# Nyquist bin on token partitions with small float32 products, and a third tree with fetched leaves

## Chip, cores and metric

The kernel runs on one core of a Trainium2 chip. The metric is device microseconds of one execution, the median of several runs.

## The reference, cut to what matters

```python
x = x + attn(layernorm(x))            # x: (2, 4096, 512)
x = x + ffn(layernorm(x))
# attn: q, k, v = unit_projection(x @ W.T + b), unit_projection(v) = ifft(fft(v) / (|fft(v)| + 1e-8)).real
#       s = cumsum(bind(k, v), axis=1); out = ifft(fft(s) * conj(fft(q))).real
# ffn:  logits = x @ W_in.T + b_in    # 8 trees of 255 nodes, depth 7
#       each tree is walked from its root, right where the logit is positive; only the 8 nodes on
#       the way keep silu(logit), the others are zero; out = masked @ W_out.T
```

In the frequency domain the attention is elementwise. Its 512 real inputs give 255 complex bins and two real ones, bin 0 and bin 256. Bin 256 is called the Nyquist bin, or in the code before `special` and `sp_`.

## The kernel before, in words

8192 tokens go through in 32 blocks of 256 (`T`), each as two halves of 128 tokens (`J` = 2). `steps` runs a set-up (`first`), the first block, a loop over blocks 1 to 30 and the last block. Every engine has its instructions in an order written out by hand in its own `step(i, attn, nxt)`; block i's feed-forward part is interleaved with the attention part of block n = i + 1 and with the first layer norm of block n + 1. Engines synchronise by semaphores, and each executes strictly in its order.

TensorE (`step`, L597): `project` for Q, K and V (L477, 144 products of 256 columns); `logits` of eight trees (L507), each in up to two column groups of 128 nodes, twelve products of 256 columns a group; `counts` (L517), which adds to a tree's logits a large negative number for every node off the path, from the decisions `dec`; `leaf_rows_of` (L526); `down` for both token halves (L542, products of 512 columns; three for every column group); and `inverse_transform` of block n (L477, bank_i). The float32 values are split into fp16 high and low halves, hence three products each.

Trees in `GATHERED` (0 and 1) have only their inner nodes in the dense product, `DENSE` = 14 column groups in all. Their one leaf for each token is found by `leaf` (L709), `leaf_rows_of` and `leaf_row_copy` (L720), fetched by an indirect DMA on GpSimd (`fetch`, L1027), multiplied with the token on VectorE (`leaf_dots`, L1199), passed through silu (`leaf_silu`, L730) and added (`leaf_add`, L1209).

The Nyquist bin lies before on single partitions: ScalarE's `evac_im` (L684 to L688) writes row 32q of `sp_raw`, 256 tokens along the row. VectorE adds eps (L1123), inverts (L1125), multiplies (`special_unit`, L1131, L1134), scans (`special_sum`, L1154) and splits (`special_product`, L1166 to L1170); TensorE adds it to the inverse transform by two one-row products for each half (`tab_sp`, in L477).

Around these VectorE does the `residual` (L1222 to L1234), the statistics and normalisation of layer norm (L1056 to L1088), the reciprocals of q and of k times v (L1098, L1110), `decide` (L1179, from logits to `dec`), `act_low` (L1186, the low halves of activations), the scans (L1142, L1145) and `result` (L1240). ScalarE evacuates projections, squares, takes roots (L701), does `silu` (L742) and `act_high` (L752). GpSimd does `sum_squares` (L935), `add_eps`, `q_unit`, `bind` (L958 to L961), `unbind` (L968 to L971), `z_sums`, `z_low` (L983) and the fetches. SyncE transposes normalised tokens by DMA (`xt` for the projections, `x2t` for the logits).

## Time and profile before

| what | us |
|---|---|
| median of 3 runs | 1993.65 |
| lowest, highest | 1991.71, 1995.52 |
| the profiled execution | 1992.84 |
| its span, first to last instruction | 1991.0 |

A block is read in the timelines from one first product of Q's projection to the next. The profile has 39541 instructions; the mean granted TensorE clock is 0.987 of full. Matmuls are pipelined: the timeline prints the length of each instruction or group, but what one costs TensorE is the distance from its start to the start of the next. "Idle" in brackets is the time that the engine sat idle before, with what ended it.

### The profile page before, as it was taken

The numbers are of one execution on the slowest core, as the hardware profiler recorded it, in microseconds if no ns is written. First come the engines' busy times: TensorE is split into PE (matmuls) and PEld (weight loads), VectorE is DVE, ScalarE is ACT, GpSimd is POOL, SyncE is SP. The second block draws the span as 40 slices with busy tenths as digits, with TensorE's granted clock in tenths as the row PEclk, the third lists the DMA queues.
The fourth block names the chain that finished last, engine by engine and source line by source line (L and its number), as shares of the span: only waits on it lengthen the run. The fifth ranks groups of instructions, "written<-read, shape, count | busy, mean of one in ns | idle before, by whom it ended". The sixth has DMA issues, their size and how long they took to land.

```text
span 1991.0 us, 39541 instructions
## 1 busy us (share of the span) xinstructions
PE 1868.4 (94%) x14360; PEld 1362.3 (68%) x14360; DVE 1744.3 (88%) x2900; ACT 1131.1 (57%) x2150; POOL 945.9 (48%) x744
## 2 busy tenths in 40 slices
PE   8489999999999999999999999999999999999978
PEld 6367766677766667766667776667776666776655
DVE  4988899988899889899988889998889998889983
ACT  5565555566555566555556555556655555655533
POOL 1354454554444554445555445455444555544540
PEclk9699999999999999999999999999999999999998
DMA  8022232222232222223222223222223322222312
GB/s 272 11 75 76 74 95 74 74 84 74 74 95 91 67 79 76 78 84 95 65 83 84 74 74 95 74 74 90 69 74 95 93 65 79 79 76 83 85 54 64
DMA packets 181642, 163.05 MB, mean 82 GB/s; under 512 B 140146, under 2 KB 140658, under 8 KB 181618
## 3 DMA queue, kind: packets, MB, share of 16 engines
q1 hardware_dynamic: 163186, 95.35, 16.6%
q0 software_dynamic: 18432, 67.38, 10.9%
q8 instruction: 15, 0.25, 0.1%
q14 instruction: 9, 0.07, 0.0%
HBM read 95.58 MB, written 16.78 MB: 56 GB/s over the span
## 4 chain that ended last, share of the span: by engine, by line
DVE 57%; issue 16%; PE 9%; POOL 5%; ACT 4%; DMA 2%; DVEq 1%; SPq 1%; POOLq 0%; ACTq 0%
DVE arena L1186 9%; PE bank_l L507 7%; DVE sp_hat L1131 6%; DVE arena L1209 4%; DVE arena L1199 4%; DVE sp_den L1125 3%; DVE dec L1179 3%; DVE xn_pair L1088 2%; DVE sp_cum L1154 2%; DMA arena<-xn_pair 2%; DVE arena L1142 2%; DVE st L1056 2%; DVE sp_den L1123 2%; DVE arena L1145 2%; DVE arena L1110 2%
## 5 line engine op out<-in xcount | busy, mean ns | idle before, releaser
L507 PE MATMUL bank_l<-arena,win_mem 128*128 128x256 f16 x5376 | 625.7, 273 | 27.4 <-DMA arena<-xn_pair 27.4
L542 PE MATMUL bank_l<-wout_mem,arena 128*128 128x512 f16 x2688 | 590.8, 379 | 0.3 <-DVE arena L1186 0.3
L507 PEld LDWEIGHTS bank_l<-arena,win_mem 128*128 128x128 f16 x5376 | 522.0, 98 | 96.5 <-issue 19.1
L477 PE MATMUL bank_p<-arena,wf_hi 128*128 128x256 f16 x3072 | 508.5, 273 | 18.0 <-DMA arena<-xn_pair 9.9
L542 PEld LDWEIGHTS bank_l<-wout_mem,arena 128*128 128x128 f16 x2688 | 263.0, 98 | 304.0 <-DVE arena L1186 0.8
L477 PE MATMUL bank_p<-arena,wf_lo 128*128 128x256 f16 x1536 | 419.3, 273 | 0.0
L935 POOL TENSOR_TENSOR arena<-arena 128x512 f32<-128x512 f32 x96 | 121.7, 1268 | 617.7 <-ACT arena L697 617.7
L477 PEld LDWEIGHTS bank_p<-arena,wf_hi 128*128 128x128 f16 x3072 | 296.1, 98 | 65.1 <-ACT arena L688 16.7
L742 ACT ACTIVATE arena<-bank_l,bias_in,s_logit 128x256 f32<-128x256 f32 x448 | 225.8, 558 | 168.1 <-PE bank_l L517 167.7
L1186 DVE SCALAR_TENSOR_TENSOR arena<-arena,s_act 128x512 f16<-128x512 f32 (+1 forms) x256 | 252.5, 1006 | 39.6 <-ACT arena L752 39.5
L1179 DVE TENSOR_SCALAR dec<-bank_l,thr,off 128x256 bf16<-128x256 f32 x256 | 131.9, 527 | 64.5 <-PE bank_l L507 64.2
L1027 POOL DMA_INDIRECT arena<-in_leaf_rows,leaf_row x128 | 149.2, 1166 | 66.0 <-ACT leaf_row L720 36.5
L752 ACT ACTIVATE arena<-arena,s_act 128x512 f16<-128x512 f32 (+1 forms) x256 | 162.7, 662 | 1.0
L477 PEld LDWEIGHTS bank_p<-arena,wf_lo 128*128 128x128 f16 x1536 | 150.6, 98 | 17.7
L730 ACT ACTIVATE leaf_act<-leaf_dot,arena 128x1 f32<-128x1 f32 x128 | 30.7, 287 | 230.1 <-DVE arena L1199 230.1
L958 POOL TENSOR_TENSOR arena<-arena 128x512 f32<-128x512 f32 x31 | 44.2, 1426 | 189.9 <-DVE arena L1116 189.9
L517 PE MATMUL bank_l<-dec,path 128*128 128x256 bf16 x512 | 98.7, 274 | 37.1 <-DVE dec L1179 33.5
L1131 DVE TENSOR_TENSOR sp_hat<-sp_raw,sp_den 1x256 f32<-1x256 f32 x93 | 124.0, 1333 | 0.8
L677 ACT ACTIVATE arena<-bank_p,bias_f 128x256 f32<-128x256 f32 x192 | 80.0, 468 | 70.5 <-PE bank_p L477 70.5
L1110 DVE RECIPROCAL arena<-arena 128x256 f32<-128x256 f32 x64 | 111.7, 1747 | 1.1
L983 POOL TENSOR_TENSOR arena<-arena 128x512 f16<-128x512 f32 x62 | 98.0, 1601 | 23.1 <-ACT arena L665 23.1
L1098 DVE RECIPROCAL arena<-arena 128x256 f32<-128x256 f32 x64 | 107.6, 1721 | 0.0
(180 smaller groups left out, 2722.3 us busy)
## 6 DMA issues: line engine op xcount, KB each, us to landing
arena<-in_x SPq DMA_DIRECT2D x32, 512.0 KB, 3.6
arena<-arena SPq DMA_DIRECT2D x32, 512.0 KB, 2.9
out<-arena SPq DMA_DIRECT2D x64, 256.0 KB, 2.1
wout_mem<-in_w_in_t SPq DMA_DIRECT2D x1, 3584.0 KB, 15.1
arena<-in_w_out_t SPq DMA_DIRECT2D x1, 3584.0 KB, 14.1
arena<-xn_pair SPq DMA_TRANSPOSE x128, 2.7
arena<-in_leaf_rows,leaf_row POOLq DMA_INDIRECT x128, 4.9
win_mem<-in_wq SPq DMA_DIRECT2D x1, 1024.0 KB, 8.3
```

The source lines that it names most:

```text
L477: mm = pe.matmul(bank, a, b, start=(n == 0), stop=(n == len(pairs) - 1))
L507: mm = pe.matmul(bank_l[t % 4][:, c * T:(c + 1) * T], a[:, k, w:w + P], x2t[:, :, b, k, :], start=(c == 0 and k == 0 and m == 0), stop=((t ...
L542: mm = pe.matmul(bank_l[j][:, :], a[:, m, tok], w[:, m, :], start=(m == 0 and a is a_hi and w is wout_hi), stop=(m == DENSE - 1 and a is a ...
L742: ins = act.activation(acts[:, t % HELD, c * T:(c + 1) * T], bank_l[t % 4][:, c * T:(c + 1) * T], ACT.Silu, bias=bias_in[:, c, t:t + 1], s ...
L752: act.activation(a_hi[:, m:m + wide, :], acts[:, t % HELD, 0:wide * T].rearrange("p (c t) -> p c t", c=wide), ACT.Copy, scale=s_act[:, 0:1 ...
L935: pool.tensor_tensor(mag[:, q].rearrange("p c t -> p (c t)"), sq[:, 0:2].rearrange("p c t -> p (c t)"), sq[:, 2:4].rearrange("p c t -> p ( ...
L1027: pool.indirect_dma_start(fetched[:, g, j, :], None, leaf_rows, bass.IndirectOffsetOnAxis(leaf_row[:, g, j:j + 1], 0)).then_inc(leaf_fetch ...
L1098: dve.reciprocal(mag[:, Q, h], mag[:, Q, h]).then_inc(rinv_ready, 1)
L1110: dve.reciprocal(mag[:, V, h], mag[:, V, h]).then_inc(kv_rinv_ready, 1)
L1131: ins = dve.tensor_tensor(sp_hat[0:1, q, :], sp_raw[s, :], sp_den[s, :], ALU.mult)
L1179: dve.tensor_scalar(dec[:, t % HELD, :], bank_l[t % 4][:, 0:T], thr[:, t:t + 1], off[:, 0:1], ALU.is_gt, ALU.mult).then_inc(dec_ready, 1)
L1186: dve.scalar_tensor_tensor(out=a_lo[:, m, :], in0=acts[:, t % HELD, 0:wide * T].rearrange("p (c t) -> p c t", c=wide), scalar=s_act[:, 0:1 ...
```

## The change

A third tree (2) goes to `GATHERED`; `DENSE` becomes 13, and its leaves have a fetch round of their own (`leaf_rows_of(i, 1)`, `leaf_row_copy(i, 1)`, `fetch(i, 2)`, `leaf_dots(i, 2)`, `leaf_silu(i, 2)`, `leaf_add(i, 2)`). The Nyquist bin is turned by TensorE onto token partitions, [128 tokens, 2 halves, 3], by two float32 products on `sp_raw` (`nyquist_rows`); size, eps, inverse, unit and product are six-element instructions; its running sum is five float32 products with an upper triangle and a full matrix (`nyquist_sums`). It no longer goes through the inverse transform: `residual` adds it per token as a scalar, added on even and subtracted on odd positions, for which the columns are sorted by parity. The four one-row products of `tab_sp` go. The orders on TensorE, ScalarE, GpSimd and VectorE are written anew.

```diff
-GATHERED = (0, 1)
+GATHERED = (0, 1, 2)
 LEAVES = len(GATHERED)
-ROUNDS = ((0, 1),)
+ROUNDS = ((0, 1), (2,))
...
-        tab_sp = sb("tab_sp", [1, QI + 2], F16)
+        running = sb("running", [P, 2 * P + 3])
+        upper, full, row_of = running[:, 0:P], running[:, P:2 * P], running[0:96, 2 * P:2 * P + 3]
...
                         f = (2 * part + c) * P
                         pairs = []
 
             def logits(i, t, c):
 
+                if c == 0 and t == 0:
+                    pe.wait_ge(x2t_ready, 16 * J * (i + 1))
...
+            def nyquist_rows(n):
+
+                pe.wait_ge(raw_im, 3 * n + 3)
+                if not isinstance(n, int) or n:
+
+                    pe.wait_ge(x1_ready, J * n)
+                for j in range(J):
+                    mm = pe.matmul(sp_rows[:, j, :], sp_raw[:, j * P:(j + 1) * P], row_of, start=True, stop=True)
+                mm.then_inc(sp_rows_full, 1)
+
+            def nyquist_sums(n):
+
+                pe.wait_ge(sp_kv_ready, n + 1)
+                pe.matmul(sp_sums[:, 0:1], upper, sp_kv[:, 0:1], start=True, stop=True)
+                pe.matmul(sp_sums[:, 1:2], upper, sp_kv[:, 1:2], start=True, stop=False)
+                pe.matmul(sp_sums[:, 1:2], full, sp_kv[:, 0:1], start=False, stop=True)
+                pe.matmul(sp_sums[:, 2:3], full, sp_kv[:, 0:1], start=True, stop=False)
+                pe.matmul(sp_sums[:, 2:3], full, sp_kv[:, 1:2], start=False, stop=True).then_inc(sp_sums_full, 1)
...
+                if rnd:
+                    pe.wait_ge(leaf_row_ready, len(ROUNDS) * i + rnd)
...
-                        if t == LEAVES:
+                        if t == 3:
...
+            def transform_back(i):
+
+                n = i + 1
+                pe.wait_ge(z_hi_ready, 2 * n + 2)
+                pe.wait_ge(z_lo_ready, 2 * n + 2)
+
+                pe.wait_ge(leaf_row_ready, len(ROUNDS) * (i + 1))
+                pe.wait_ge(sp_carry_ready, n + 1)
+                for j in range(J):
+                    pe.wait_ge(x1_ready, J * i + j + 1)
+                    inverse_transform(j)
...
-                    if c == 0:
-                        pairs += [(sp_z_hi[:, tok], tab_sp[:, :]), (sp_z_lo[:, tok], tab_sp[:, :])]
...
+                nyquist_rows(0)
...
-
-                    pe.wait_ge(xt_ready, 16 * J * (n + 1))
-                    pe.wait_ge(raw_im, 3 * n)
                     project(n, Q)
                     project(n, K)
                     project(n, V)
...
+                    nyquist_rows(n)
+                logits(i, 0, 0)
+                logits(i, 1, 0)
+                counts(i, 0)
+                logits(i, 2, 0)
+                logits(i, 3, 0)
+                logits(i, 3, 1)
+                logits(i, 4, 0)
+                logits(i, 4, 1)
+                counts(i, 1)
+                if attn:
+                    nyquist_sums(n)
+                leaf_rows_of(i, 0)
+                counts(i, 2)
+                counts(i, 3)
+                logits(i, 5, 0)
+                logits(i, 5, 1)
+                leaf_rows_of(i, 1)
+                logits(i, 6, 0)
+                counts(i, 4)
+                logits(i, 6, 1)
+                logits(i, 7, 0)
+                counts(i, 5)
+                logits(i, 7, 1)
+                counts(i, 6)
+                down(i, 0)
+                down(i, 1)
+                if attn:
+                    transform_back(i)
...
+            def nyquist_size(n):
+
+                act.wait_ge(sp_rows_full, n + 1)
+                act.activation(sp_size, sp_rows, ACT.Abs).then_inc(sp_abs_ready, 1)
...
+                if q == Q and (not isinstance(n, int) or n):
+
+                    act.wait_ge(sp_rows_full, n)
...
+                act.activation(root_warm[:, :], ln_eps[:, :], ACT.Sqrt)
                 if attn:
                     evac_re(n, Q)
                     evac_im(n, Q)
+                    evac_re(n, K)
                     square(n, Q)
-                    evac_re(n, K)
                 std(i, mv2, rs2, ln2_mv, ln2_std)
                 if attn:
-                    root(n, Q)
+                    evac_im(n, K)
                 if attn:
 
...
-                    evac_im(n, K)
+                    root(n, Q)
+                    evac_re(n, V)
                     square(n, K)
-                    evac_re(n, V)
+                    evac_im(n, V)
                     root(n, K)
-                    evac_im(n, V)
+                    nyquist_size(n)
                     square(n, V)
-                if isinstance(i, int) and i == 0:
-
-                    act.wait_ge(ffn_consts_done, 1)
-                leaf(i, 0)
-                if attn:
                     root(n, V)
                 if nxt:
                     std(n + 1, mv1, rs1, ln1_mv, ln1_std)
-                if attn:
-                    sp_magnitude()
-                leaf(i, 1)
+                if isinstance(i, int) and i == 0:
+
+                    act.wait_ge(ffn_consts_done, 1)
+                leaf(i, 0)
...
                 silu(i, 0)
+                act_high(i, 0)
+                leaf(i, 1)
                 silu(i, 1)
+                leaf_row_copy(i, 0)
+                leaf(i, 2)
                 silu(i, 2)
-                act_high(i, 0)
                 act_high(i, 1)
+                act_high(i, 2)
                 silu(i, 3)
-                act_high(i, 2)
                 act_high(i, 3)
-                leaf_row_copy(i, 0)
-                silu(i, 4)
-                act_high(i, 4)
-                silu(i, 5)
-                silu(i, 6)
-                act_high(i, 5)
...
+                silu(i, 4)
+                silu(i, 5)
+                act_high(i, 4)
+                act_high(i, 5)
+                silu(i, 6)
+                silu(i, 7)
+                act_high(i, 6)
                 act_high(i, 7)
+                leaf_silu(i, 0)
+                leaf_row_copy(i, 1)
                 if attn:
                     z_high(n)
-                leaf_silu(i, 0)
                 leaf_silu(i, 1)
-                if attn:
-                    act.activation(root_warm[:, :], ln_eps[:, :], ACT.Sqrt)
+                leaf_silu(i, 2)
...
+                    add_eps(n, K)
+                    sum_squares(n, V)
                     q_unit(n)
-                    sum_squares(n, V)
...
                     z_sums(n)
+                fetch(i, 2)
+                if attn:
                     z_low(n, 0)
                     z_low(n, 1)
...
+            def nyquist_den(n):
 
                 dve.wait_ge(sp_abs_ready, n + 1)
-                dve.tensor_scalar(sp_den[:, :], sp_den[:, :], eps_sp[:, 0:1], None, ALU.add).then_inc(spd_ready, 1)
...
+                dve.tensor_tensor(sp_den[:, :, :], sp_size, eps_sp[:, :, :], ALU.add).then_inc(sp_den_ready, 1)
+
...
+            def nyquist_unit(n):
+
                 dve.wait_ge(sp_inv_ready, n + 1)
...
+                dve.tensor_tensor(sp_hat[:, :, :], sp_rows, sp_den[:, :, :], ALU.mult).then_inc(sp_hat_ready, 1)
+
+            def nyquist_bind(n):
+
                 dve.wait_ge(sp_hat_ready, n + 1)
-                dve.tensor_tensor(sp_kv[:, :], sp_hat[:, K, :], sp_hat[:, V, :], ALU.mult).then_inc(sp_kv_ready, 1)
+                dve.tensor_tensor(sp_kv[:, :], sp_hat[:, :, K], sp_hat[:, :, V], ALU.mult).then_inc(sp_kv_ready, 1)
+
+            def nyquist_unbind(n):
+
+                dve.wait_ge(sp_sums_full, n + 1)
+                dve.scalar_tensor_tensor(out=sp_z[:, :], in0=sp_sums[:, 0:J], scalar=sp_carry[:, 0:1],
+                                         in1=sp_hat[:, :, Q], op0=ALU.add, op1=ALU.mult).then_inc(sp_z_ready, 1)
+
+            def nyquist_carry(n):
+
+                dve.wait_ge(sp_z_ready, n + 1)
+                dve.tensor_scalar(sp_carry[:, :], sp_sums[:, J:J + 1], sp_carry[:, 0:1], keep[:, bass.ds(n + 1, 1)],
+                                  ALU.add, ALU.mult).then_inc(sp_carry_ready, 1)
...
+            def carries(n):
+
                 dve.wait_ge(cum_ready, n + 1)
-                dve.wait_ge(sp_cum_ready, n + 1)
-
-                kp = keep[:, bass.ds(n + 1, 1)]
-                dve.tensor_scalar(carry[:, :], cum[:, :, T - 1], kp, None, ALU.mult).then_inc(carry_ready, 1)
-                dve.tensor_scalar(sp_carry[:, :], sp_cum[:, T - 1:T], keep[0:1, bass.ds(n + 1, 1)], None,
+                dve.tensor_scalar(carry[:, :], cum[:, :, T - 1], keep[:, bass.ds(n + 1, 1)], None,
                                   ALU.mult).then_inc(carry_ready, 1)
...
                 cos, sin = xn2[:, j, 0:2 * QI], xn2[:, j, 2 * QI:4 * QI]
                 xj, edge = x1[:, j, :], 4 * QI
-                dve.tensor_tensor(cos[:, 0:QI], ce[:, 0:QI], co[:, 0:QI], ALU.add)
-                dve.tensor_tensor(cos[:, QI:], ce[:, 0:QI], co[:, 0:QI], ALU.subtract)
+                dve.wait_ge(sp_z_ready, i + 1)
+                top, odds, evens = sp_z[:, j:j + 1], slice(0, ODDS), slice(ODDS, QI)
+                for part, sign in ((odds, ALU.subtract), (evens, ALU.add)):
+                    up, down = cos[:, part], cos[:, QI + part.start:QI + part.stop]
+                    dve.scalar_tensor_tensor(out=up, in0=ce[:, part], scalar=top, in1=co[:, part], op0=sign, op1=ALU.add)
+                    dve.scalar_tensor_tensor(out=down, in0=ce[:, part], scalar=top, in1=co[:, part], op0=sign,
+                                             op1=ALU.subtract)
...
                     wout_low(3)
                 if attn:
                     q_inverse(n, 0)
-                    q_inverse(n, 1)
                 if nxt:
                     next_stats(n + 1)
+                if attn:
+                    nyquist_den(n)
+                    nyquist_inverse(n)
+                    nyquist_unit(n)
                 decide(i, 0)
-                decide(i, 1)
-                if attn:
+                if attn:
+                    q_inverse(n, 1)
                     kv_denominator(n)
                     kv_inverse(n, 0)
+                    kv_inverse(n, 1)
+                    nyquist_bind(n)
+                    k_scale(n)
+                decide(i, 1)
                 decide(i, 2)
-                if attn:
-                    kv_inverse(n, 1)
-                    k_scale(n)
+                decide(i, 3)
                 act_low(i, 0)
-                decide(i, 3)
                 decide(i, 4)
-                act_low(i, 1)
-                act_low(i, 2)
-                act_low(i, 3)
-                decide(i, 5)
-                decide(i, 6)
-                if attn:
-                    running_sum(n)
-                act_low(i, 4)
                 if nxt:
                     scale_and_shift(n + 1)
+                if attn:
+                    nyquist_unbind(n)
+                decide(i, 5)
+                act_low(i, 1)
+                if attn:
+                    running_sum(n)
+                act_low(i, 2)
+                decide(i, 6)
+                if attn:
+                    nyquist_carry(n)
+                act_low(i, 3)
                 decide(i, 7)
+                act_low(i, 4)
                 act_low(i, 5)
-                if attn:
-                    special_inverse(n)
                 act_low(i, 6)
                 act_low(i, 7)
-                if attn:
-                    special_unit(n)
+                leaf_dots(i, 0)
+                leaf_add(i, 0)
                 if nxt:
                     low_of(n + 1, 0, xn1, xn1_hi_ready, xn1_lo_ready)
-                if attn:
-                    special_sum(n)
-                leaf_dots(i, 0)
-                if attn:
-                    special_product(n)
-                if nxt:
                     low_of(n + 1, 1, xn1, xn1_hi_ready, xn1_lo_ready)
                 leaf_dots(i, 1)
-                leaf_add(i, 0)
+                if attn:
+                    carries(n)
                 leaf_add(i, 1)
+                leaf_dots(i, 2)
+                leaf_add(i, 2)
                 result(i, 0)
                 result(i, 1)
 
```

## Rows read from the trace of the kernel before

**Rows 1.** The page: busy us (share of the span) and instructions of each engine.

```profile
PE 1868.4 (94%) x14360; PEld 1362.3 (68%) x14360; DVE 1744.3 (88%) x2900; ACT 1131.1 (57%) x2150; POOL 945.9 (48%) x744
```

**Rows 2.** Windows, 200 to 1800 us: engines busy us; granted clock (1.00 full).

```profile
200.00:1800.00 1600.00, 1545.49 (x12015) 1125.14 (x12014) 1445.40 (x2383) 925.85 (x1789) 805.64 (x626) 1.00 0.27 80
```

**Rows 3.** TensorE timeline, one block: start us, us, line, operation [idle <-releaser].

```profile
986.47 0.39 PE L477 MATMUL bank_p<-arena,wf_hi 128*128 128x256 f16 x2 [0.43 <-DMA arena<-xn_pair]
...
1002.43 0.27 PE L477 MATMUL bank_p<-arena,wf_lo 128*128 128x256 f16 x1
1003.24 0.39 PE L507 MATMUL bank_l<-arena,win_mem 128*128 128x256 f16 x2 [0.53 <-DMA arena<-xn_pair]
...
1020.71 0.39 PE L517 MATMUL bank_l<-dec,path 128*128 128x256 bf16 x2 [0.21 <-DVE dec L1179]
...
1023.77 1.46 PE L542 MATMUL bank_l<-wout_mem,arena 128*128 128x512 f16 x6
1025.99 0.39 PE L517 MATMUL bank_l<-dec,path 128*128 128x256 bf16 x2 [0.75 <-DVE dec L1179]
...
1043.05 0.22 PE L477 MATMUL bank_i<-tab_hi,arena 128*128 128x129 f16 x1
...
1045.62 0.39 PE L477 MATMUL bank_p<-arena,wf_hi 128*128 128x256 f16 x2 [0.41 <-DMA arena<-xn_pair]
```

**Rows 4.** The same timeline, the inverse transform of one token half.

```profile
1043.16 0.22 PE L477 MATMUL bank_i<-tab_hi,arena 128*128 128x129 f16 x1
1043.32 0.23 PE L477 MATMUL bank_i<-tab_sp,sp_z_hi 1*128 1x129 f16 x1
...
1043.53 0.23 PE L477 MATMUL bank_i<-tab_hi,arena 128*128 128x128 f16 x1
```

**Rows 5.** Waits of TensorE, 200 to 1800 us: total us, times, longest us.

```profile
PE bank_l L517 <- DVE dec L1179: 27.5, 50, 0.8
...
PE bank_l L507 <- DMA arena<-xn_pair: 9.4, 27, 0.7
PE bank_p L477 <- DMA arena<-xn_pair: 9.2, 22, 0.4
```

**Rows 6.** TensorE timeline, set-up: small float32 products (a call is x2).

```profile
5.38 0.57 PE L434 MATMUL bank_p<-b_pair,arena 128*128 128x6 f32 x2
5.81 0.57 PE L429 MATMUL bank_p<-b_pair,arena 128*128 128x6 f32 x2
...
20.91 0.28 PE L443 MATMUL bank_l<-mx,arena 128*128 128x5 f32 x2
21.05 0.68 PE L455 MATMUL bank_i<-arena 128*128 128x257 f32 x2
```

**Rows 7.** ScalarE timeline: evacuation of Q's imaginary part after its last product.

```profile
991.92 0.47 ACT L684 ACTIVATE sp_raw<-bank_p,bias_f 1x256 f32<-1x256 f32 x1 [1.78 <-PE bank_p L477]
...
992.74 0.45 ACT L688 ACTIVATE arena<-bank_p,bias_f 128x256 f32<-128x256 f32 x1
```

**Rows 8.** VectorE groups, whole span: busy us, mean ns | idle before.

```profile
L1131 DVE TENSOR_TENSOR sp_hat<-sp_raw,sp_den 1x256 f32<-1x256 f32 x93 | 124.0, 1333 | 0.8
...
L1125 DVE RECIPROCAL sp_den<-sp_den 96x256 f32<-96x256 f32 x32 | 56.0, 1749 | 1.1
...
L1123 DVE TENSOR_SCALAR sp_den<-sp_den,eps_sp 96x256 f32<-96x256 f32 x32 | 43.1, 1347 | 0.4 <-ACT sp_den L835 0.4
```

**Rows 9.** VectorE timeline: low halves of activations, GpSimd busy, then idle.

```profile
1016.74 3.46 DVE L1186 SCALAR_TENSOR_TENSOR arena<-arena,s_act 128x512 f16<-128x512 f32 x2 [1.11 <-ACT arena L752]
...
1023.61 0.72 DVE L1186 SCALAR_TENSOR_TENSOR arena<-arena,s_act 128x512 f16<-128x512 f32 x1
```

**Rows 10.** VectorE timeline: first instruction of the residual.

```profile
1048.56 0.29 DVE L1222 TENSOR_TENSOR arena<-bank_i,odd 128x127 f32<-128x127 f32 x1 [0.29 <-DVE arena L1240]
```

**Rows 11.** GpSimd timeline: second fetch of leaves; low half of z.

```profile
1029.80 1.25 POOL L1027 DMA_INDIRECT arena<-in_leaf_rows,leaf_row  x1 [0.15 <-issue]
...
1035.60 3.05 POOL L983 TENSOR_TENSOR arena<-arena 128x512 f16<-128x512 f32 x2 [0.74 <-ACT arena L665]
```

192 lines of the change are left out of this document (76 added, 116 removed).

## The prediction

> **What bounds the kernel now.** I read the page's busy shares first: TensorE 94%, VectorE 88% [rows 1]. The stretch from 200 to 1800 us shows the steady state: TensorE is busy 1545 of 1600 us, VectorE 1445, at full clock [rows 2]. Then I read one block in TensorE's timeline [rows 3], from the first product of Q's projection at 986.47 to the next one at 1045.62: 59.15 us. The reader is to see that products follow one another almost without a gap, with four small idle spots: 0.70 us between the last projection product (1002.43 plus one step of 0.11) and the first logits (1003.24), which wait for the transposed tokens; 0.21 and 0.75 us ahead of `counts`, which wait for a decision on VectorE; 0.41 us ahead of the next projection, again for transposed tokens. The waits view gives them over 27 blocks: 27.5 us for decisions, or 1.0 a block, and 9.4 and 9.2 us for the two transposes [rows 5]. So TensorE is the bound; VectorE, second at 90%, causes most of the gaps. What TensorE is spared is gained, unless VectorE's or another engine's new order takes it back.
>
> **The change part by part, for one block.** The sum is made on TensorE.
>
> Logits: one column group less, 12 products. 143 steps of projection, same shape, take 1002.43 - 986.47 = 15.96 us, 0.11 each [rows 3]; so -1.3 us. Down: 84 products become 78. From 1023.77 to 1043.05 are 19.28 us; less 0.75 of stall and 0.22 of `counts` that is 18.31, or 0.218 each; so -1.3. The one-row products: from 1043.16 to 1043.53 [rows 4] the last ordinary product and the two of them take 0.37 us, where an ordinary one takes about 0.06 (two from 1043.05 [rows 3] to 1043.16); 0.31 for each half, -0.6 for both. Two more leaf-row products: at most an ordinary 0.06 each, +0.1.
>
> Five float32 products for the sums. The trace has small ones in the set-up only. At 5.38 a call with six columns takes 0.43 us to the next, at 20.91 one with five columns takes 0.14 [rows 6]. The second was preceded by a wait, in which its weights could be loaded; the first ones follow one another, but at the very start. These are the ends: 0.7 to 2.2 us for five. I take 0.21, as the 20.91 one is at the clock of the steady state, and a back-to-back call can't hide its second load: +1.05.
>
> The Trainium skill speaks against this part: "TensorE: Matmul & The Clock Gate", section on weight-path perf modes, says that the fast weight load does not apply to fp32 weights; and "FP8 and Floating Point Precision", TensorE Precision Notes, has true fp32 as four passes. The doubled instructions of the rows fit in kind, while two instructions a call are not four. By a full unhidden load the price would be that of the upper end, the rival named below.
>
> `nyquist_rows` sits between projection and logits and waits for ScalarE to evacuate V's imaginary part. For Q this evacuation starts at 991.92 and its third instruction starts at 992.74 and lasts 0.45 [rows 7]; Q's last product ends near 991.8 (48 steps of 0.11 after 986.47), so the data are there 1.4 us after it; with the semaphore 1.5. Then come two float32 calls, 0.4. Against today's gap of 0.70 that is +1.2. Ends: +0.9 if ScalarE is quicker, +2.2 if `square(n, K)`, ahead of it in its queue, runs late. Behind this wait stand all logits. The wait for transposed tokens, which ends the gap now, is hidden under it as long as VectorE's chain from the inverse transform to the transposes isn't over 1.3 us later.
>
> That chain: `residual` starts at 1048.56 now [rows 10], 3.5 us after the inverse transform's end, since VectorE is behind. The change takes three unit products of 1.33 us, an inversion of 1.75 and an addition of 1.35 [rows 8] from it, with the scan and splits some 10 us a block, and gives back an estimated 1.5 us of six-element instructions, four operations on 128x512 for `leaf_dots` and `leaf_add` at some 0.7 each as the shorter one in [rows 9], and an estimated 0.3 to 1.1 for the residual, whose two 0.29 us operations for each half [rows 10] become four of half the length. VectorE falls from 53 (0.903 of 59.15 [rows 2]) to about 47 us a block. Costed at nothing on the path: it is hidden by TensorE, as is the third leaf on ScalarE; SyncE's queue keeps its order. The transposes of the next block's tokens come earlier, as their low halves no longer stand behind the Nyquist work: the 0.34 us stall (9.2 us over 27) goes.
>
> The stalls at `counts`, 1.0 us a block, go in their present places: `counts(7)` now has three trees, not two, of `down` ahead of it, and the others are a group later. New ones come. VectorE's new order puts both inversions of k and v (as long as that of [rows 8], 3.5 us) and k's scaling ahead of `decide(1)`; worked through with present durations, `decide(1)` ends about 0.65 us after TensorE wants it for `counts(1)`. And five `act_low` (trees 3 to 7) and `decide(7)` must fit between the scans and the end of the first half of `down`. One takes 0.72 us when GpSimd is idle, 1.73 beside its `bind` (3.46 for two) [rows 9]; TensorE takes 1.3 a tree. I take 0.35 of stall, bounds 0 and 1.8. GpSimd gets a third fetch (1.25 plus about 1.1 and gaps, 2.7 us) ahead of `z_low`, which now ends at 1038.65, 4.4 us before it is needed [rows 3, 11]; `down` ends 1 to 2 us sooner, so near 1 us of cover is left. Cost nothing; if `bind` starts over 1 us later, every further us counts.
>
> The Trainium skill's "GPSIMD Engine Reference", table of specifications, says that GpSimd shares SBUF interfaces with VectorE, where the latter has two SBUF inputs. The 0.72 against 1.73 agrees. It leaves the new products with a PSUM input alone.
>
> Sum: -1.3 - 1.3 - 0.6 + 0.1 + 1.05 + 1.2 = -0.85; -0.34 - 1.0 of stalls gone, +0.65 + 0.35 new: -1.2 a block. With 31 blocks -37 us.
>
> Ends of the run: the last block has no attention; it gains logits and down, 2.6. In the set-up the addition and the inversion stand once on the path to the first inverse transform (1.35 + 1.75 by the means) [rows 8], about -3 with the small ones that replace them and the smaller weights to split. Together -43; 1992.84 - 43 = 1949.8. The median of the runs is 0.8 above the profiled execution: 1950.
>
> **The rivals.**
>
> A, the forecast: 1950, by its stalls of about 1 us a block 1935 to 1965.
>
> B, no new stall: both new ones vanish, since VectorE has 7 us a block to spare and can be ahead of TensorE. 31 x 1.0 less: 1919. For it speaks the idle time that VectorE gains; against it that GpSimd's instructions stretch VectorE's.
>
> C, starved `down`, on the slower side: `silu(7)` waits for `act_low(4)`, `act_high(6)` stands behind `silu(7)`, and `act_low(6)` behind that. If each `act_low` costs 1.73 beside GpSimd's `unbind` and fetches, the five stretch 5 us beyond the short ones; what `down` can't hide is 1.8 us, and with z then late behind the third fetch 1 more. Against the 0.35 that is +2.45 a block: 1950 + 76 = 2026. It decides from 1.4 us above my stalls; up to there the change still gains. For it: the 1.73. Against: the 0.72, whenever GpSimd happens to wait.
>
> D, loads of float32 weights unhidden: 0.43 for each of seven calls, +1.5 a block: 1950 + 48 = 1998, no change. For it the row at 5.38; against it the clock and place of that row.
>
> E, the evacuation is not the end of that wait, but the transposes, by a residual that is 1.1 us longer: +0.3 to 0.8 a block, 1960 to 1975. Still faster.
>
> **How the numbers follow.** A 0.45, B 0.22, C 0.13, D 0.08, E 0.12. Range 1915 to 1998: from B with some block terms smaller, to D; C lies outside and a tail below B. A measurement of this kernel can tell 0.2%, 4 us, from no change. Faster: A, B, E and a little of D, 0.80; same: half of D and a sliver of C, 0.05; slower 0.15.
>
> **What would show each step right or wrong.** TensorE's timeline: first logits about 2 us after V's last product, released by ScalarE; the float32 group of five about 1.05 us long; `down` starting at once, and `counts(7)` without wait. The waits view: decisions under 1.0 us a block together with waits for L1186's successor. VectorE busy about 47 of 58. GpSimd's `z_low` ends before `down` does. The block from projection to projection near 57.9 us. Wrong would be: waits of `down` for low halves over 1 us a block, or the inverse transform waiting for GpSimd.

## The result, and the profile after

The changed kernel takes 2117.1 us (median of 4, 2111.4 to 2121.3), the one before 1992.7 (median of 4 on the same chip): ratio 1.063, 95% interval 1.059 to 1.066. It is 124 us slower where 43 us less were forecast.

From the page of the kernel after, the busy line of the engines and the two DMA kinds (number, median us from issue to landing), then its steady state and three shorter stretches as windows (columns as in [rows 2]; the last three are granted clock, DMA engines' busy share and GB/s):

```profile
PE 1881.7 (89%) x14168; PEld 1400.7 (66%) x14168; DVE 1623.7 (77%) x3066; ACT 1116.6 (53%) x2247; POOL 987.7 (47%) x800
```

```profile
arena<-xn_pair SPq DMA_TRANSPOSE x128, 3.8
arena<-in_leaf_rows,leaf_row POOLq DMA_INDIRECT x192, 6.1
```

```profile
200.00:1900.00 1700.00, 1545.15 (x11792) 1149.92 (x11791) 1332.17 (x2505) 906.40 (x1857) 835.81 (x673) 0.95 0.40 91
1039.90:1058.20 18.30, 16.07 (x144) 13.93 (x144) 15.20 (x40) 12.81 (x28) 3.22 (x3) 1.00 0.37 106
1058.20:1064.00 5.80, 4.87 (x31) 3.82 (x32) 2.77 (x8) 2.51 (x5) 1.96 (x2) 0.71 0.15 27
1103.00:1107.00 4.00, 3.92 (x21) 2.90 (x22) 3.23 (x6) 2.62 (x6) 0.00 (x0) 0.57 0.00 0
```

Against [rows 1, 2]: 192 instructions less, and yet TensorE is busy longer; its idle share rises from 3.4% to 9%; the granted clock falls from 1.00 to 0.95, and the last two rows show where: behind waits of TensorE, where the mean of the stretch lies between the two levels (1.2 and 2.4 GHz), 0.71 and 0.57 of 2.4. It does not happen behind every wait: the row from 1039.90 starts behind one of 2.96 us and stands at 1.00. The DMA engines' busy share rises from 0.27 to 0.40 with 14% more bytes a second. VectorE falls only from 53 to 49.5 us a block (1332.17 of 1700, times 63.13), not to 47.

The waits of the kernel after, 200 to 1900 us, 27 blocks (total us, times, longest us):

```profile
DVE arena L1236 <- DMA arena<-in_leaf_rows,leaf_row: 107.8, 27, 5.7
PE bank_p L480 <- DMA arena<-xn_pair: 105.4, 27, 5.6
PE bank_i L551 <- ACT arena L740: 44.0, 27, 1.9
PE bank_l L530 <- DMA arena<-xn_pair: 4.1, 7, 0.9
```

The waits for decisions in [rows 5] have gone. In their place TensorE waits 3.9 us a block for the transposed tokens of the next block (0.34 before), and 1.6 for V's imaginary part. The same in TensorE's timeline, one block:

```profile
1039.95 0.39 PE L480 MATMUL bank_p<-arena,wf_hi 128*128 128x256 f16 x2 [2.96 <-DMA arena<-xn_pair]
1058.23 0.60 PE L551 MATMUL bank_i<-running,sp_raw 96*128 96x3 f32 x4 [1.94 <-ACT arena L740]
1059.73 4.18 PE L530 MATMUL bank_l<-arena,win_mem 128*128 128x256 f16 x24 [0.90 <-DMA arena<-xn_pair]
1063.97 6.71 PE L530 MATMUL bank_l<-arena,win_mem 128*128 128x256 f16 x60
1070.75 0.28 PE L557 MATMUL bank_i<-sp_kv,running 128*128 128x1 f32 x2
...
1071.57 0.36 PE L561 MATMUL bank_i<-sp_kv,running 128*128 128x1 f32 x2
1103.08 0.39 PE L480 MATMUL bank_p<-arena,wf_hi 128*128 128x256 f16 x2 [3.62 <-DMA arena<-xn_pair]
```

From projection to projection 63.13 us, 3.98 more than in [rows 3]; times 31 that is 123, the whole loss. In this block, by the terms of the prediction: the wait ahead of the projection +3.2 (3.62 for 0.41; forecast -0.34); from the end of V's last product (1056.13) to the logits 3.60 for 0.70, so +2.9 (forecast +1.2); the first 24 logits products take 4.02 us (to 1063.75), not the 2.6 that 24 of the sixty behind them take, +1.4 (not forecast); the float32 group +1.04 (from 1070.75 to 1071.57 and a call of 0.22); waits at `counts` and `down` -1.0; work removed -3.2, as forecast. That makes 4.4; 0.4 is unassigned. This block is one of the slower ones at the logits. Over the 13 blocks from 600 to 1400 us the first 24 products of the projection take 2.63 us in four blocks and 3.8 to 5.1 in nine of them; the first 24 of the logits 2.6 in five and 3.9 to 4.3 in eight: 2.2 us a block more than at the full clock.

Why the transposes are late shows on GpSimd, SyncE and VectorE just ahead of that block (the third pair of fetches and `z_low` behind it, the transposes' issue, VectorE):

```profile
1028.05 1.23 POOL L1063 DMA_INDIRECT arena<-in_leaf_rows,leaf_row  x1 [0.16 <-POOL arena L1027]
1029.58 0.95 POOL L1063 DMA_INDIRECT arena<-in_leaf_rows,leaf_row  x1 [0.30 <-issue]
1030.55 2.27 POOL L1034 TENSOR_TENSOR arena<-arena 128x512 f16<-128x512 f32 x2
```

```profile
1029.80 3.51 SPq L339 DMA_TRANSPOSE arena<-xn_pair  x2
```

```profile
1024.48 0.68 DVE L1236 SCALAR_TENSOR_TENSOR arena<-arena 128x512 f32<-128x512 f32 x1
...
1030.24 3.13 DVE L1236 SCALAR_TENSOR_TENSOR arena<-arena 128x512 f32<-128x512 f32 x1
...
1039.03 0.69 DVE L1236 SCALAR_TENSOR_TENSOR arena<-arena 128x512 f32<-128x512 f32 x1 [3.00 <-DMA arena<-in_leaf_rows,leaf_row]
...
1044.31 0.28 DVE L1263 SCALAR_TENSOR_TENSOR arena<-bank_i,sp_z,odd 128x64 f32<-128x64 f32 x1 [0.41 <-DVE arena L1284]
```

The transposes are issued 1.8 us behind the first gather of the third pair, and the last of both kinds land near 1039, some 9 us after their issue (9.3 for the second gather, 8.7 and 9.3 for the transposes; the first gather takes 5.3). VectorE waits for the fetch, and the residual begins at 1044.31, 7.3 us after the end of the inverse transform (1039.95 less 2.96), against 3.4 before by the same reckoning ([rows 10] less 1045.21 of [rows 3]). How long the transposes take from issue to landing (minimum, median, maximum over 200 to 1900 us), first before, then after; half of them are those of `xn2`, which meet no fetch:

```profile
DMA to landing us min/median/max: 2.7/2.8/4.2
```

```profile
DMA to landing us min/median/max: 3.1/5.4/12.0
```

### The profile page after: what moved, and what is told of

Read it like the earlier page. It is cut to its first block, busy times and chain, and to the rows that moved or that the text cites. A ratio compares the mean times of both kernels' runs of the same rounds, so it can differ in the third digit from the quotient of the medians.

```text
span 2109.6 us, 40048 instructions
## 1 busy us (share of the span) xinstructions
PE 1881.7 (89%) x14168; PEld 1400.7 (66%) x14168; DVE 1623.7 (77%) x3066; ACT 1116.6 (53%) x2247; POOL 987.7 (47%) x800
## 4 chain that ended last, share of the span: by engine, by line
PE 56%; DMA 16%; DVE 9%; issue 6%; ACT 6%; SPq 2%; POOL 1%; DVEq 0%; ACTq 0%; POOLq 0%
PE bank_l L530 27%; PE bank_p L480 21%; DMA arena<-xn_pair 13%; PE bank_l L590 3%; PE bank_l L540 3%; DMA arena<-in_leaf_rows,leaf_row 3%; DVE arena L1236 2%; SPq L339 2%; DVE arena L1246 2%; ACT arena L794 1%; DVE arena L1223 1%; DVE xn_pair L1126 1%; ACT arena L804 1%; ACT arena L738 1%; ACT sp_raw L736 1%
## 5 line engine op out<-in xcount | busy, mean ns | idle before, releaser
L480 PE MATMUL bank_p<-arena,wf_hi 128*128 128x256 f16 x3072 | 554.8, 288 | 117.1 <-DMA arena<-xn_pair 116.1
L530 PEld LDWEIGHTS bank_l<-arena,win_mem 128*128 128x128 f16 x4992 | 498.4, 101 | 95.7 <-DMA arena<-xn_pair 18.6
L590 PE MATMUL bank_l<-wout_mem,arena 128*128 128x512 f16 x2496 | 549.2, 379 | 0.0
L986 POOL TENSOR_TENSOR arena<-arena 128x512 f32<-128x512 f32 x96 | 121.5, 1266 | 697.1 <-ACT arena L749 697.1
L1236 DVE SCALAR_TENSOR_TENSOR arena<-arena 128x512 f32<-128x512 f32 x192 | 199.1, 1072 | 124.6 <-DMA arena<-in_leaf_rows,leaf_row 124.6
L1063 POOL DMA_INDIRECT arena<-in_leaf_rows,leaf_row x192 | 209.8, 1093 | 91.0 <-issue 46.1
L1246 DVE SCALAR_TENSOR_TENSOR arena<-arena,leaf_act 128x512 f32<-128x512 f32 x192 | 194.2, 1052 | 55.5 <-ACT leaf_act L782 55.5
L1223 DVE SCALAR_TENSOR_TENSOR arena<-arena,s_act 128x512 f16<-128x512 f32 (+1 forms) x256 | 215.0, 860 | 28.0 <-ACT arena L804 28.0
L761 ACT ACTIVATE on_leaf<-bank_l,one,off_inv 128x256 f16<-128x256 f32 x96 | 53.9, 561 | 156.7 <-PE bank_l L540 156.6
L991 POOL TENSOR_SCALAR arena<-arena,eps_s 128x512 f32<-128x512 f32 x64 | 46.5, 726 | 130.8 <-ACT arena L753 130.8
## 6 DMA issues: line engine op xcount, KB each, us to landing
wout_mem<-in_w_in_t SPq DMA_DIRECT2D x1, 3328.0 KB, 16.3
```

The lines of the kernel that those rows point to most:

```text
L480: mm = pe.matmul(bank, a, b, start=(n == 0), stop=(n == len(pairs) - 1))
L530: mm = pe.matmul(bank_l[t % 4][:, c * T:(c + 1) * T], a[:, k, w:w + P], x2t[:, :, b, k, :], start=(c == 0 and k == 0 and m == 0), stop=((t ...
L590: mm = pe.matmul(bank_l[j][:, :], a[:, m, tok], w[:, m, :], start=(m == 0 and a is a_hi and w is wout_hi), stop=(m == DENSE - 1 and a is a ...
L986: pool.tensor_tensor(mag[:, q].rearrange("p c t -> p (c t)"), sq[:, 0:2].rearrange("p c t -> p (c t)"), sq[:, 2:4].rearrange("p c t -> p ( ...
L1063: pool.indirect_dma_start(fetched[:, g, j, :], None, leaf_rows, bass.IndirectOffsetOnAxis(leaf_row[:, g, j:j + 1], 0)).then_inc(leaf_fetch ...
L1223: dve.scalar_tensor_tensor(out=a_lo[:, m, :], in0=acts[:, t % HELD, 0:wide * T].rearrange("p (c t) -> p c t", c=wide), scalar=s_act[:, 0:1 ...
```

## Experiments

Theory C (collision): leaf fetches and token transposes in flight together delay each other, and the projection waits behind that. Rival S (series): the third leaf's arithmetic on VectorE makes the residual late. Rival W: the wait ahead of `nyquist_rows` is what costs. Times are medians, with the ratio to the kernel before on the same chip and its 95% interval; a point is one per cent of the time of the kernel before. The lists of waits show the largest rows unless said otherwise.

### e1_low_early: the transposes issued earlier

```diff
@@ VectorE, step @@
                 act_low(i, 4)
+                low_of(n + 1, 0, ...); low_of(n + 1, 1, ...)
                 act_low(i, 5)
...
                 leaf_add(i, 0)
-                low_of(n + 1, 0, ...); low_of(n + 1, 1, ...)
```

> The changed kernel, with VectorE's two low halves of the next block's tokens moved from behind leaf_add(0) to behind act_low(4), so that SyncE issues the token transposes before the second and third leaf fetches are in flight. Theory C (collision: transposes and leaf fetches in flight together delay each other): TensorE's wait ahead of the projection, 3.9 us a block in the changed kernel, falls under 0.5, transposes land in about 3 us, the clock returns towards 1.00, and the time is 1950 to 2010 us. Theory W (the waits and float32 products of the Nyquist part in TensorE's own order cost the time): the order of this pair changes little, 2090 to 2120. Theory S (the third leaf makes VectorE late by itself): the wait ahead of the projection goes, but the one ahead of the logits grows, 2060 to 2110.

2048.9 us, 1.031 [1.024, 1.039]: 3.1 points of the 6.3 are back. The wait of the projection for transposes is gone; 1.3 us a block of waiting for ScalarE (`evac_im`, L740) stand there now, and ScalarE's square root ahead of it waits 3.0 us a block (79.9 over 27) for VectorE, whose residual is late. C's range (1950 to 2010) is missed by 39 us: the collision carries half of the loss, and something else the rest.

### e2_no_third_fetch, e3_nyquist_only, e4_tree_only: the parts alone

e2 puts a `memset` of one column in place of the third fetch (the third tree's leaf is missing from its output). e3 keeps two gathered trees and takes the Nyquist part with the new orders. e4 is the kernel before with the third gathered tree alone, its fetch between `z_sums` and `z_low`.

```diff
@@ e2: GpSimd, fetch @@
-                for j in range(J): pool.indirect_dma_start(fetched[:, 2, j, :], ...)
+                for j in range(J): pool.memset(no_fetch[:, j:j + 1], 0.0)
@@ e3 @@
-GATHERED = (0, 1, 2)
+GATHERED = (0, 1)
```

> The changed kernel without the DMAs of the third leaf fetch (each is a GpSimd memset of one column, and the rows stay zero, so the third tree's leaf is left out of the output); every other instruction is there. Theory C: transposes land in 3 to 4 us, waits ahead of the projection under 0.5 us a block, 1950 to 1990 us. Theory S: also 1950 to 1990, since VectorE no longer waits for the third leaf; C and S are told apart by the run with the early low halves. Theory W: 2090 to 2120, GpSimd being off the path.

> The changed kernel with its Nyquist part and its new orders, but only two gathered trees (14 column groups, two fetches). TensorE has 2.6 us a block more work than in the changed kernel. Theories C and S: no third fetch, so the wait ahead of the projection is small; 1990 to 2040 us. Theory W: the loss of the Nyquist part stays and the dense column comes on top, 2150 to 2210.

> The kernel before with the third gathered tree alone: its Nyquist part and its orders stay as before, the third fetch stands between z_sums and z_low. Theory C: the first of the two transposes, issued near the third fetch, is late, the second is not; VectorE, fuller by 2.5 us a block, is late for the residual: 2000 to 2100 us. Theory W: TensorE is spared 2.5 us a block and nothing is added to it: 1920 to 1950.

e2: 1987.1, 1.000 [0.997, 1.003]. e3: 1992.3, 1.003 [1.002, 1.004]. e4: 2126.9, 1.071 [1.067, 1.074]. The waits of TensorE (200 to 1850 us) of e2, all of them, then the largest of e4:

```profile
PE bank_i L552 <- ACT arena L741: 52.9, 28, 1.9
PE bank_l L531 <- DMA arena<-xn_pair: 20.6, 28, 1.2
```

```profile
PE bank_p L477 <- DMA arena<-xn_pair: 70.8, 26, 4.5
```

Without the third fetch the wait for tokens is not in the list, with the rest of the change in place; with the third tree alone it is. So the third gathered tree loses the time, the Nyquist part neither loses nor gains (W falls as the cause of the loss: its wait of 1.9 us stands in e2 too, at 1.000). e4 lies 27 us above its range of 2000 to 2100; e2 and e3 lie in theirs. e2 says one thing more: it keeps the arithmetic of the third leaf on VectorE and spares TensorE 2.6 us a block, by an estimate 4 points, and still ends level with e3. So in these orders, and without its fetch, the third leaf costs about what it saves.

### e5_low_copy_early, e6_rows_late, e7_all_three

e5 is e1 with `leaf_row_copy(1)` moved ahead of `leaf_silu(0)`, behind `act_high(5)`, so that the third fetch starts earlier. e6 is the changed kernel with `nyquist_rows` behind the first two logits (and ScalarE's and VectorE's share of it moved back). e7 is both.

```diff
@@ e6: TensorE, step @@
                 project(n, V)
-                nyquist_rows(n)
                 logits(i, 0, 0)
                 logits(i, 1, 0)
+                nyquist_rows(n)
```

> The run with early low halves, and ScalarE's leaf_row_copy(1) moved from behind leaf_silu(0) to behind act_high(5), so that GpSimd can issue the third fetch at once after z_sums (it waited 2.6 us there). Theory C+S (both the collision and VectorE's wait for the third leaf cost time): the leaf lands 2.5 us sooner, VectorE reaches the residual 2 to 3 us sooner, the wait ahead of the logits and the wait of the projection for ScalarE (33.6 us over 26 blocks) go; 1.5 to 3 us a block, 1955 to 2005 us. Theory C alone: no more than 0.5 us a block, 2030 to 2050.

> The changed kernel with nyquist_rows moved on TensorE from ahead of the logits to behind the logits of trees 0 and 1, and the size, eps, inverse and unit of the bin moved back with it on ScalarE and VectorE. The wait for V's evacuation (1.9 us a block) and the lower clock in the logits behind it go, unless the transposed tokens end that wait anyway (they came 0.8 us later still in the changed kernel). Theory C: here they do, and the gain is 0 to 0.5 us a block: 2095 to 2120. Theory W: 2 to 3.5 us a block, 2010 to 2050.

> Early low halves, early leaf_row_copy and late nyquist_rows together. If the three losses (collision, VectorE's wait for the third leaf, wait for V's evacuation with its lower clock) add up to the whole distance, TensorE's 2.6 us a block of spared work should show: 1910 to 1960 us, under the kernel before (1986 on this chip). If a further cost of the third leaf stays: 1970 to 2010.

e5: 2035.1, 1.022 [1.018, 1.026], in the range of "C alone" and not in the one that was expected. e6: 2127.8, 1.069 [1.065, 1.072], no gain on the changed kernel and 8 us above C's range: its waits moved from `nyquist_rows` to the logits, which wait for `xn2`'s transposes (63.7 us over 26 blocks). e7: 2019.1, 1.014 [1.011, 1.018], above both of its ranges. What is left in e7, TensorE's largest wait, its timeline, VectorE's and one row of GpSimd's:

```profile
PE bank_l L530 <- DMA arena<-xn_pair: 89.3, 27, 3.7
```

```profile
1012.10 5.30 PE L530 MATMUL bank_l<-arena,win_mem 128*128 128x256 f16 x24 [3.45 <-DMA arena<-xn_pair]
```

```profile
1041.61 3.29 DVE L1239 SCALAR_TENSOR_TENSOR arena<-arena 128x512 f32<-128x512 f32 x1
...
1046.17 3.65 DVE L1249 SCALAR_TENSOR_TENSOR arena<-arena,leaf_act 128x512 f32<-128x512 f32 x2 [0.65 <-ACT leaf_act L784]
...
1058.28 0.28 DVE L1266 SCALAR_TENSOR_TENSOR arena<-bank_i,sp_z,odd 128x64 f32<-128x64 f32 x1 [0.41 <-DVE arena L1287]
```

```profile
1041.86 1.28 POOL L1029 TENSOR_TENSOR arena<-arena 128x512 f32<-128x512 f32 x1
```

Here no transfer is late. The three leaves run one behind another on VectorE from 1041.61 to the results near 1057.9, 16 us, some of it stretched (3.29 us, beside GpSimd's `z_sums`, for a dot product that takes 0.68 by itself), and the logits pay: 3.3 us of waiting a block and then, in eight of the 13 blocks from 600 to 1400 us, 24 products in 3.9 to 5.1 us (5.09 here) in place of 2.6.

### e8_nyquist_rows_late and e9_two_trees_std_early: the Nyquist part made to pay

e8 is e3 with `nyquist_rows` late. e9 adds ScalarE's order for the second norm; it computes everything, with two gathered trees.

```diff
@@ e9: ScalarE, step @@
                     evac_im(n, Q)
-                    evac_re(n, K)
                     square(n, Q)
                 std(i, mv2, rs2, ln2_mv, ln2_std)
-                    evac_im(n, K)
+                    evac_re(n, K)
                 act.wait_ge(xt_ready, 16 * J * (n + 1))
                 high(i, xn2, ln2_done, xn2_hi_ready)
+                    evac_im(n, K)
```

> The run with two gathered trees, and nyquist_rows late as above. There the wait for V's evacuation (1.6 us a block) is the only long wait of TensorE, and tokens are transposed in time. If that wait is the price of the Nyquist part: 0.8 to 1.6 us a block less, 1940 to 1970 us. If the transposed tokens or decide(0) end the wait instead: 1985 to 1995.

> The two-tree kernel with nyquist_rows behind the first logits, and on ScalarE the square root of the second norm (std) and the copy of the high half (high) set ahead of the work on K: order evac_im(Q), square(Q), std, evac_re(K), high, evac_im(K). In the trace of its parent std started 2.4 us after VectorE had the variances (1042.85 to 1045.22), and the logits waited 1.75 us a block for x2's transposes. Theory (the chain residual, norm, transposes ends the wait ahead of the logits, and a queue position on ScalarE is part of it): the wait of the logits goes to below 0.3 us a block, 28 x 1.6 = 45 us less than 1977, so 1925 to 1940. Rival (project(V) waits for evac_im(K) instead, or VectorE's work ends the next wait): the 1.7 us turn up ahead of the projection of V or at the counts, 1965 to 1980.

e8: 1976.9, 0.992 [0.990, 0.995], between its two ranges. e9: 1944.2, 0.981 [0.979, 0.982]: faster than both kernels, 4 us above its range. ScalarE and VectorE in e8, where the square root waits in its queue behind K's evacuation, then ScalarE in e9:

```profile
1045.22 0.29 ACT L696 ACTIVATE rs<-mv,ln_eps 128x2 f32<-128x2 f32 x1
...
1047.46 1.15 ACT L723 ACTIVATE xn_pair<-arena 128x512 f16<-128x512 f32 x2
```

```profile
1045.54 0.17 DVE L1102 RECIPROCAL rs<-rs 128x2 f32<-128x2 f32 x1 [2.70 <-ACT rs L696]
```

```profile
1025.56 0.28 ACT L696 ACTIVATE rs<-mv,ln_eps 128x2 f32<-128x2 f32 x1
1025.86 0.84 ACT L728 ACTIVATE arena<-bank_p,bias_f 128x256 f32<-128x256 f32 x2
1027.38 1.15 ACT L723 ACTIVATE xn_pair<-arena 128x512 f16<-128x512 f32 x2 [0.68 <-DVE arena L1106]
```

In e8 TensorE waits 1.75 us a block for `xn2`'s transposes. In e9 that is gone, and this is all that TensorE waits for between 200 and 1850 us, with the window of its steady state:

```profile
PE bank_l L540 <- DVE dec L1215: 19.7, 28, 0.7
```

```profile
200.00:1800.00 1600.00, 1580.35 (x12620) 1197.65 (x12619) 1312.60 (x2418) 929.45 (x1830) 837.89 (x635) 1.00 0.27 82
```

It is the 0.65 us at `counts(1)` that the prediction worked out, in its place.

### e12_spare_fetch and e14_spare_low_early: the collision by itself

e12 is e8 with a third pair of fetches into a buffer that nobody reads, issued where the changed kernel issues its third (ScalarE's `leaf_row_copy` waits for it, but only in the next block, before it writes the row numbers anew). e14 moves in addition `low_of` of the next tokens as e1 does.

```diff
@@ e12: GpSimd, step @@
                     z_sums(n)
+                for j in range(J):
+                    pool.indirect_dma_start(spare[:, j, :], None, leaf_rows, ...leaf_row[:, 1, j:j + 1]...)
                     z_low(n, 0)
```

> The two-tree kernel with nyquist_rows late (1977), plus a third pair of indirect fetches of the same size, issued where the changed kernel issues its third one, into a buffer that nobody reads: same traffic, no work and no wait on any other engine behind it. Collision theory: the median landing of the transposes rises from 2.7 us to 4 or more, the projection gets a wait for transposed tokens of 1 to 3 us a block, and the time becomes 2010 to 2070. Rival (the transfers share without loss, only VectorE's work for the third leaf costs): transposes stay below 3.2 us and the time within 1 per cent of 1977.

> The two-tree kernel with the spare third pair of fetches (2134, against 1977 without), and the low halves of the next tokens, and so the token transposes, moved ahead on VectorE, from behind the first leaf's addition to behind act_low(4). The fetches are the same, only the transposes start some 8 us sooner. Collision theory: the transposes land in 3 to 3.5 us, the wait of the projection is gone, 1980 to 2010. Rival (the spare fetch costs by itself, through GpSimd's 2.5 us and VectorE beside it, not by meeting the transposes): above 2080.

e12: 2133.7, 1.076 [1.074, 1.079], 8.4 points above e8. e14: 1992.0, 1.002 [1.001, 1.003], 7.5 points below e12 again. The issue of the spare fetch and of the transposes, then the landing of all transposes in the steady state and what TensorE waits for; e12:

```profile
1046.23 1.22 POOL L1073 DMA_INDIRECT spare<-in_leaf_rows,leaf_row  x1 [0.16 <-POOL arena L1030]
```

```profile
1047.98 2.89 SPq L341 DMA_TRANSPOSE arena<-xn_pair  x2
```

```profile
DMA to landing us min/median/max: 2.7/5.6/12.0
```

```profile
PE bank_p L482 <- DMA arena<-xn_pair: 94.7, 26, 4.8
```

and e14, with the same fetches:

```profile
1032.48 1.23 POOL L1073 DMA_INDIRECT spare<-in_leaf_rows,leaf_row  x1 [0.16 <-POOL arena L1030]
```

```profile
1026.09 2.91 SPq L341 DMA_TRANSPOSE arena<-xn_pair  x2
```

```profile
DMA to landing us min/median/max: 2.7/2.7/2.8
```

Last the DMA engines in one block, with two pairs of fetches and one pair of transposes in each: the changed kernel, all of it and from the issue of the transposes on; then e14:

```profile
1022.80:1039.10 16.30, 14.19 (x84) 7.06 (x82) 12.17 (x18) 2.38 (x8) 9.13 (x8) 1.00 0.83 158
1029.80:1039.10 9.30, 7.19 (x52) 3.89 (x49) 5.82 (x9) 0.48 (x2) 2.99 (x3) 1.00 1.09 164
```

```profile
1026.00:1039.50 13.50, 13.17 (x62) 5.82 (x61) 12.51 (x16) 3.64 (x10) 10.28 (x9) 1.00 0.64 195
```

Nobody reads the spare rows and no work in the block stands behind them. The transposes issued 1.8 us behind them take up to 12 us; issued 6.4 us ahead of them, never over 2.8. This shows C: it is neither the traffic nor GpSimd's time, which both remain in e14 (together they cost 0.9 points against e8), but the meeting. The order counts: in e14 the two transposes are issued at 1026.1 and 1027.8 and the second pair of fetches at 1027.3 and 1028.8, as near as in e12, and they are not late. In e12, as in the changed kernel, two pairs of fetches are ahead of them; no run puts them right behind one pair only.

The last three rows show what the mean of 0.40 hides. While both kinds are in flight the 16 engines are full (1.09; the share adds up the times of packets). The bytes are nearly the same, 158 times 16.3 is 2.6 MB and so is 195 times 13.5, but the engines spend 13.5 us on them (0.83 of 16.3) where e14 spends 8.6 (0.64 of 13.5). Together the packets take longer, then; by which mechanism stays open.

The size was missed: 2134 for an expected 2010 to 2070. Against e8 that is 157 us, or 5.1 a block. TensorE waits 3.6 us for the tokens of the projection, where 1 to 3 were expected, and the next 24 products take 1.2 us more than in e8 on average (2.63 to 5.1 us over the 13 blocks from 600 to 1400 us). VectorE's wait for ScalarE's square root grows too, to 7.5 us a block (195.7 over 26, 2.7 in e8), as it stands behind the evacuations of a late projection; TensorE does not feel that, it waits 1.75 us for `xn2`'s transposes in both.

The Trainium skill, "DMA: Bandwidth & Descriptors", section on queues, rings and completion order, says that a DMA engine takes packets from its queues in turn, and that the increment which reports a transfer is written only after all earlier writes of that engine, those of other queues too. The trace agrees in kind: the second gather and the transposes issued near 1029 are reported late, near 1039, while by themselves they land in 2.7 and 4.5 to 5.6 us (e8). No run here tells a late write from a late report of it.

### e10, e11, e13, e15: the series on VectorE

e10 is e7 with e9's ScalarE order. e11 is the changed kernel and e13 is e10, each with the third tree's dot product and addition over one column, not 512 (so that the third leaf is left out of the output but for one column; fetch and waits stay). e15 is e7 with the leaves in the order dots 0, dots 1, add 0, dots 2, add 1, add 2 and `high` ahead of `evac_im(K)`.

```diff
@@ e11, e13: leaf_dots and leaf_add, g == 2 @@
-                    row = fetched[:, g, j, 0:D]
+                    row = fetched[:, g, j, 0:1]
@@ e15: VectorE, step @@
-                leaf_add(i, 0)
                 leaf_dots(i, 1)
+                leaf_add(i, 0)
-                leaf_add(i, 1)
                 leaf_dots(i, 2)
+                leaf_add(i, 1)
                 leaf_add(i, 2)
```

> The three-tree kernel with all three edits (low halves of the next tokens early, leaf_row_copy(1) early, nyquist_rows late), and the same order of std and high on ScalarE as in the two-tree one. Its parent ran at 2019 and waited 3.4 to 3.7 us a block ahead of the logits. Theory: 2 us of that goes and with it part of the slow products behind it: 28 x 2 to 2.8 = 55 to 80 us less, 1940 to 1965; what is left of the wait, 1.4 us, is the third leaf's series on VectorE. Rival (the late residual alone sets it, ScalarE's place doesn't matter since the residual is late): above 2005.

> The changed kernel, but the third tree's dot product and its addition on VectorE run over one column instead of 512, so that the third leaf is missing from the output but for one column; its fetch, with all waits for it, stays. Collision theory (fetches and token transposes in flight together delay each other, and everything behind the transposes waits): transposes and fetches land as late as in the changed kernel (medians above 5 and 6 us), the projection still waits over 3 us a block; four operations of about 0.7 us each are saved on the way to the residual, 2.8 us, which can pay only behind the logits' wait of 0.9 us a block: 2060 to 2110. Serial theory (the third leaf's arithmetic on VectorE is the cost): 1985 to 2030.

> The three-tree kernel with all edits and std and high early (2081), and the third tree's dot product and addition over one column instead of 512, so that its leaf is missing from the output but for one column; fetch and waits stay. In its parent VectorE reaches the residual some 3.5 us after the inverse transform, std waits 4.4 us for it on ScalarE, and K's evacuation stands behind std. Theory (with the collision gone, VectorE's series of three leaves is the rest of the cost): about 2.8 us less in the series; the residual starts under 1 us late, the waits of the projection for ScalarE (2.7 us a block) vanish, and the work taken from TensorE (2.6 us a block) counts: 1880 to 1930, below the two-tree kernel's 1944. Rival (the fetches themselves still delay something, by traffic or by the queue): over 1960.

> The complete three-tree kernel with low halves, leaf_row_copy(1) and nyquist_rows moved (2019), the leaves on VectorE in the order dots 0, dots 1, add 0, dots 2, add 1, add 2, so that no addition stands directly behind the dot product whose ScalarE value it needs (0.6 us of idle time for each leaf), and on ScalarE high ahead of evac_im(K), with std left where it was. Theory (series on VectorE): 1.2 to 1.8 us less in the series and up to 1 us from high, against a wait of 3.4 us a block ahead of the logits: 1955 to 1985. Rival (the third fetch lands too late for dots 2, so that the series ends when it ended): 2005 to 2025.

e11: 2093.4, 1.056 [1.054, 1.059]: while the collision stands, the arithmetic is worth 0.7 points; the projection waits 104.5 us in 27 blocks as before. e10: 2080.7, 1.050 [1.048, 1.052], worse than e7, against the expectation. e13: 1959.7, 0.986 [0.983, 0.988]: with the collision gone, the same four short operations are worth 6.4 points. e15: 2066.2, 1.039 [1.035, 1.043], worse than e7 and outside both of its ranges.

What e10 waits for, on TensorE over 200 to 1850 us (its largest wait) and on ScalarE in one block, then all of e13's waits of TensorE:

```profile
PE bank_p L480 <- ACT arena L728: 72.4, 27, 2.7
```

```profile
1035.76 0.30 ACT L696 ACTIVATE rs<-mv,ln_eps 128x2 f32<-128x2 f32 x1 [4.39 <-DVE mv L1104]
```

```profile
PE bank_l L540 <- DVE dec L1220: 37.8, 28, 1.4
PE bank_l L530 <- DMA arena<-xn_pair: 27.1, 28, 1.3
PE bank_l L590 <- DVE arena L1227: 18.9, 28, 0.7
```

An early place on ScalarE pays only if VectorE is on time. In e10 the residual is late, the square root stands 4.39 us at the head of the queue, and K's evacuation behind it holds the projection. That is the price of an order: e9 gains 1.1 points by it, e10 loses 3.6. So the 6.4 points between e10 and e13 hold for this order; in e7's no run takes the four operations away. e15 fell for the same reason (the projection waits 57.5 us in 27 blocks for `evac_im(K)` behind `high`) and for one that its expectation hadn't: `leaf_dots(1)`, now ahead of `leaf_add(0)`, waits up to 3.9 us for the second fetch. e13 missed its range from above: four operations less, VectorE is still 1.3 us late at worst for the logits, 1.4 for `decide(1)`, 0.7 for `act_low`. That is 3.0 us a block by its three rows (83.8 us over 28), more than the 2.6 that the third tree takes from TensorE.

## Why the prediction was wrong, point by point

- **TensorE's own terms held.** Float32 sums 1.04 for 1.05; the inverse transform 2.16 us (1043.05 to 1045.62 less 0.41, [rows 3]) became 1.5 (1035.47 to 1039.95 less 2.96). Rival D, unhidden loads, is out: 0.22 us a call, after a first of 0.15. The clock that the prediction held against D's row at 5.38 was no reason, though: from 5.30 to 6.30 us the kernel before shows 1.00.
- **`nyquist_rows`**: forecast +1.2, between +0.9 and +2.2. ScalarE's wait alone is 1.6 a block on average; with the products (0.6) and the logits' own wait (0.15), less the 0.53 that TensorE was idle there in [rows 3], that is +1.85, within the bounds; in the block shown it is +2.9. The value taken was too low, not the mechanism. With it the part alone makes 1.003 (e3); with the products behind the first logits 0.992 (e8).
- **The failed step: "The transposes of the next block's tokens come earlier ... the 0.34 us stall (9.2 us over 27) goes."** The second of the two came earlier, and both came right behind GpSimd's third fetch. The term was -0.3 us and is +3.6 a block on average, 31 times. The argument compared their place with the VectorE work behind which they stood, and never asked what else is in flight when they are issued. The rows for it were there: [rows 11] has the second fetch, and the change puts another directly behind.
- **The second failed step: "Costed at nothing on the path: it is hidden by TensorE", said of VectorE's chain with the leaf's four operations in it, and "Cost nothing", said of GpSimd's third fetch.** VectorE's sum over a block was near (49.5; forecast 47, where the prediction's own terms, 53.4 - 10 + 1.5 + 2.8 + 0.7, make 48), but the leaf's work stands in series between the last low half and the residual, where busy shares say nothing. e10 against e13 prices four operations of 0.7 us at 6.4 points, some 127 us or 4.1 a block, where they take 2.8 themselves; part of that is e10's order on ScalarE. e2, with the operations and without the fetch, lets them cost about the 2.6 us that TensorE is spared. GpSimd itself was on time, as forecast: no run shows the inverse transform waiting for it.
- **The stalls at `counts(1)` and `down`** (0.65 and 0.35): absent in the kernel after, since TensorE was late itself; 0.7 in e9 and 1.4 and 0.7 in e13, where it is not. Rival C's mechanism, starved `down`, did not occur: 0.7 us at most, in any run. Rival E names the right neighbour, transposes behind a late residual, and prices it at 0.3 to 0.8; with the third leaf's series it is 3.3 in e7.
- **Not in the sum at all**: behind many of the waits the next products run slow, 24 of them in 3.8 to 5.1 us for 2.6. In the block shown this adds 1.4 us, over 13 blocks 2.2 on average.
- **The account**: after to e1, the collision, 3.1 points; e1 to e5 and e7, the late third fetch and `nyquist_rows`, 1.7 (e1's interval and e5's overlap, so the division within it is loose); e7 is 1.4 above the kernel before, and e9, without the third tree, 1.9 below. What stays open: e13 shows that the rest is VectorE's series, but no run has a three-tree kernel that is on time with its whole third leaf, so whether the third tree can pay is not settled. The 0.9 points of a fetch that meets nothing (e14 against e8) were not divided between GpSimd and VectorE.
